# A quantised feed-forward kernel: 40 instead of 36 gate units finished during the up pass, with their magnitudes stored in DRAM

## The reference

```python
def act_qdq(x):
    qmax = 2.0 ** (ACT_BITS - 1) - 1.0
    scale = jnp.maximum(jnp.max(jnp.abs(x)) / qmax, 1e-12)
    return jnp.clip(jnp.round(x / scale), -qmax - 1.0, qmax) * scale
...
x = act_qdq(x)
up = act_qdq(x @ lpbq_dequant(w_up).T)
gate = act_qdq(x @ lpbq_dequant(w_gate).T)
sig = fixed_qdq_u16(jax.nn.sigmoid(gate))
gate = act_qdq(gate * sig)
o = act_qdq(gate * up)
return o @ lpbq_dequant(w_down).T
```

## Time and profile before

| | us |
|---|---|
| median of three runs | 2368.29 |
| profiled execution | 2368.93 |
| span of its trace | 2367.2 |
| TensorE busy in the span | 2019.6 |
| VectorE busy | 1708.7 |
| ScalarE busy | 1400.7 |

### The profile page before, as it was taken

How to read it: one execution, slowest core, us unless ns; L and a number is a source line. 1 busy time by engine, 2 the same in 40 slices (tenths; PEclk the granted TensorE clock), 3 DMA queues, 4 the chain that set the end, 5 groups by cost and what they waited for, 6 DMA issues and landing times.

```text
span 2367.2 us, 25402 instructions
## 1 busy us (share of the span) xinstructions
PE 2019.6 (85%) x9524; PEld 945.2 (40%) x9524; DVE 1708.7 (72%) x1372; ACT 1400.7 (59%) x1613; POOL 671.2 (28%) x665
## 2 busy tenths in 40 slices
PE   5688888888679999999999999999100699999998
PEld 2344444444334444444444444444000244444443
DVE  8699999999624534542399998999899745577641
ACT  2577878887522322232399987676899633366530
POOL 0499999999500000000022210222111000000000
PEclk9899999999889999999999999999555799999999
DMA  5879999999246755853599995787998755555541
GB/s 205 332 280 350 333 351 331 348 334 343 111 178 213 252 213 178 264 183 143 215 364 386 380 371 221 258 317 296 391 418 328 307 214 209 211 211 231 231 151 71
DMA packets 131163, 634.60 MB, mean 268 GB/s; under 512 B 12257, under 2 KB 12769, under 8 KB 91105
## 3 DMA queue, kind: packets, MB, share of 16 engines
q1 hardware_dynamic: 85888, 316.81, 36.8%
q0 software_dynamic: 45152, 316.16, 34.3%
HBM read 430.69 MB, written 202.24 MB: 267 GB/s over the span
## 4 chain that ended last, share of the span: by engine, by line
PE 63%; DVE 3%; issue 3%; ACT 2%; DMA 0%; POOL 0%; DVEq 0%; ACTq 0%; POOLq 0%
PE ff_pp L1640 42%; PE ff_pp L1654 21%; ACT ff_ring L1583 1%; DVE ff_sig L1437 1%; DVE ff_h_parts L1421 1%; DVE ff_sq L1359 1%; DMA ff_ab<-hT_scratch 0%; ACT ff_sig L1570 0%; DVE ff_sq L1428 0%; DVE kept_gate L1430 0%; DVE ff_gin L1372 0%; DVE ff_hq L1411 0%; ACT ff_hq L1494 0%; ACT ff_ring L1609 0%; ACT ff_sig L1599 0%
## 5 line engine op out<-in xcount | busy, mean ns | idle before, releaser
L1654 PE MATMUL ff_pp<-kept_down,kept_gate 128*128 128x512 f16 x1536 | 459.0, 381 | 193.1 <-DVE kept_up L1478 193.1
L1640 PE MATMUL ff_pp<-ff_h_parts,kept_gate 128*128 128x512 f16 x2304 | 499.7, 380 | 19.9 <-DVE ff_h_parts L1271 19.9
L1640 PE MATMUL ff_pp<-ff_h_parts,kept_up 128*128 128x512 f16 x2304 | 497.4, 379 | 0.0
L1501 ACT ACTIVATE ff_raw<-ff_pp 128x1024 f32<-128x1024 f32 x192 | 194.5, 1018 | 395.8 <-PE ff_pp L1640 395.8
L1640 PEld LDWEIGHTS ff_pp<-ff_h_parts,kept_gate 128*128 128x128 f16 x2304 | 225.9, 98 | 293.7 <-DVE ff_h_parts L1271 20.3
L1640 PEld LDWEIGHTS ff_pp<-ff_h_parts,kept_up 128*128 128x128 f16 x2304 | 225.4, 98 | 271.8
L1276 DVE TENSOR_REDUCE kept_gate_peak<-ff_raw 128x1 f32<-128x2048 f32 x48 | 109.7, 2286 | 292.5 <-ACT ff_raw L1501 292.5
L1654 PEld LDWEIGHTS ff_pp<-kept_down,kept_gate 128*128 128x128 f16 x1536 | 150.6, 98 | 376.0 <-issue 196.0
L1654 PE MATMUL ff_pp<-kept_down,kept_up 128*128 128x512 f16 x768 | 292.1, 380 | 0.0
L1609 ACT ACTIVATE ff_ring<-ff_hq,kept_g 128x2048 int16<-128x2048 f32 x48 | 96.0, 1999 | 191.1 <-DVE ff_hq L1411 189.7
L675 PE MATMUL at_psO<-kept_wo,at_ahi 128*128 128x512 f16 x512 | 153.9, 382 | 36.3 <-ACT at_alo L453 31.6
(11 more groups left out here) (239 smaller groups left out, 3446.7 us busy)
## 6 DMA issues: line engine op xcount, KB each, us to landing
ff_raw<-up_scratch SPq DMA_DIRECT2D x66, 1024.0 KB, 8.4
gate_scratch<-ff_raw POOLq DMA_DIRECT2D x48, 1024.0 KB, 6.5
ff_gin<-gate_scratch SPq DMA_DIRECT2D x48, 1024.0 KB, 8.8
up_scratch<-ff_raw POOLq DMA_DIRECT2D x48, 1024.0 KB, 7.0
ff_gin<-gate_integers SPq DMA_DIRECT2D x73, 512.0 KB, 6.0
gate_integers<-ff_ring POOLq DMA_DIRECT2D x43, 512.0 KB, 9.3
kept_up<-up_scratch SPq DMA_DIRECT2D x21, 1024.0 KB, 9.2
kept_xs<-in_x SPq DMA_DIRECT2D x32, 512.0 KB, 13.9
```

The lines of the kernel that those rows point to most:

```text
L1501: nc.scalar.activation(raw[:, n % UNITS, h * 2 * BLK:(h + 1) * 2 * BLK], pp[(2 * n + h) % 4][:, :, :].rearrange("p a t -> p (a t)"), ACT.C ...
L1640: mm = nc.tensor.matmul(pp[k % 4][:, h, :], wt[w][:, c, f:f + P], a[:, b % 2, :, c, :], start=(q == 0), stop=(q == len(todo) - 1))
L1654: mm = nc.tensor.matmul(pp[k % 8 // 2][:, k % 2, :], a[b % 2][:, f, t * P:(t + 1) * P], wt[w][:, f, :], start=(q == 0 and i == 0), stop=(q ...
```

## The change

READY goes from 36 to 40, so `second` starts at up unit 28 and 8 units are left "late". Magnitudes of 36 of the 40 are made in the up pass, at the unit in `MAG_AT`: two in most units from 31 on, one in unit 44, three in units 33, 46 and 47. For the 23 units that pass through the slots and are loaded again in the stretch of products (`passing`), ScalarE writes the magnitude into one of two tiles `ab`, and GpSimd's queue stores it (0.5 MB) in a new DRAM tensor behind the unit's other stores. The next magnitude in the same tile waits until that store has landed, and `load_again` waits for the magnitude before it fills a slot again. The stretch of products loads these magnitudes where it loaded integers. In it 36 units are "done", 8 "late", 3 "act" and 1 "dve" (before: 13, 12, 15 and 8).

```diff
-READY = 36
+READY = 40
...
-    DONE = list(range(KEPT)) + [v for v in range(KEPT, READY) if v - KEPT >= AGAIN - AR][:5]
     LOADED = AGAIN - AR
+    MAG_AT = {v: SECOND + ((3, 3, 4, 4, 5, 17, 18, 19)[v] if v < KEPT else v // 2 + 1 if v < KEPT + LOADED else v // 2 + 2)
+              for v in range(READY)}
+    DONE = sorted((v for v in range(READY) if MAG_AT[v] < NU), key=lambda v: (MAG_AT[v], v))
...
+        mag_out = [s.sem(f"mag_out{i}") for i in range(2)]
...
-            return [v for j, v in enumerate(DONE) if n == SECOND + max(3 + j if v < KEPT else 0, v // 2 + 2)]
+            return [v for v in DONE if MAG_AT[v] == n]
+
+        def passing(v):
+
+            return KEPT <= v < KEPT + LOADED
...
-            if made[i] == "done":
+            if home[i] == "load":
+                if made[i] == "done":
+                    have_gated(eng, i)
+                else:
+                    eng.wait_ge(m["ga_" + made[i]], nth(i) + 1)
+            elif made[i] == "done":
...
                             sp.wait_ge(again_out[w % AR], 16 * (w // AR))
+                            sp.wait_ge(m["mag"], DONE.index(KEPT + w - AR) + 1)
                         sp.dma_start(again(KEPT + w), gate_q[w]).then_inc(again_in[w % AR], 16)
...
+                def store_magnitude(v):
+                    w = v - KEPT
+                    pool.wait_ge(m["mag"], DONE.index(v) + 1)
+                    pool.dma_start(mag_d[w], ab[:, w % 2, :]).then_inc(mag_out[w % 2], 16)
...
+                        if j >= 2:
+                            pool.wait_ge(mag_out[j - 2], 16 * len(range(j - 2, LOADED, 2)))
                     if not late(u):
-                        pool.wait_ge(again_out[u % AR], 16 * (u // AR + 1))
-                    pool.dma_start(gated(i), gate_q[u]).then_inc(g_in[kind, j], 16)
+                        pool.wait_ge(mag_out[u % 2], 16 * (u // 2 + 1))
+                    pool.dma_start(gated(i), gate_q[u] if late(u) else mag_d[u]).then_inc(g_in[kind, j], 16)
...
                     for v in second_units(n - 1):
                         store_gated(v)
+                    for v in magnitude_at(n - 1):
+                        if passing(v):
+                            store_magnitude(v)
...
                 def magnitude(v):
 
+                    if passing(v):
+                        w = v - KEPT
+                        act.wait_ge(m["g2"], v + 1)
+                        if w < 2:
+                            act.wait_ge(m["gpeak"], NU)
+                        need(act, mag_out[w % 2], 16 * (w // 2))
+                        nc.scalar.activation(ab[:, w % 2, :], again(v), ACT.Abs).then_inc(m["mag"], 1)
+                        return
...
+    mag_d = nc.dram_tensor("gate_magnitudes", [NB * UNITS, P + 1, UE], I16).ap()[:, 0:P, :]
```

More of the change, by code:

```diff
@@ L772, in quantiser, with feed @@
     link(nc.vector.tensor_tensor(inv, inv, unit, ALU.mult))
-def feed(nc, keep, hT_d, hq_d, gate_d, up_d, gate_q, x1_d, out, NB, scale_d, mats):
+def feed(nc, keep, hT_d, hq_d, gate_d, up_d, gate_q, mag_d, x1_d, out, NB, scale_d, mats):
     g, al_ = keep["g"], keep["alpha"]
@@ L1702, in build @@
                     keep[n] = [keep[n + "_all"][:, i] for i in range(2)]
-                feed(nc, keep, hT_d, hq_d, gate_d, up_d, gate_q, x1_d, out, NB, scale_d,
+                feed(nc, keep, hT_d, hq_d, gate_d, up_d, gate_q, mag_d, x1_d, out, NB, scale_d,
                      [(up_n, up_t, "up", 5, F), (down_n, down_t, "down", 6, D)])
```

## The result

The changed kernel takes 2396.07 us (median of four runs, 2393.33 to 2397.33) against 2368.4, the median of four runs of the kernel before: a ratio of 1.0114 with an interval of 1.0101 to 1.0126, 27.7 us slower. The forecast was 2367 with a range up to 2382, so it was wrong in size and in sign. All three places where it put time did move, and in the directions it gave; two of the three sizes were off, both to the same side.

What follows compares the result with a forecast made beforehand. TensorE's matmuls carry the passes; in the 193.1 us hole ScalarE, VectorE and DMA engines are all full, and DMA would remain. Up pass 18, hole -24.5, restart 5 make -1.5 us: 2367, range 2353 to 2382.

Steps and rivals of the forecast that it cites:

- three places: Where the change was to count: up pass (18 us later), idle hole before the down pass (24.5 less), restart (5 more).
- The store loop: Up pass, units 34 to 44: magnitudes wait for earlier stores to land; two units take 16.2 us plus 6.5, costing 10.7.
- The block load: Up pass: `load_hq` stands behind magnitude waits, so VectorE stands some 3.5 us four times; counted half, 7 us.
- bound drawn for the lateness: Upper bound for the up pass's later end: landing 9.4, 12.8 us per unit, 26.7 + 5 = 32 us.
- The hole: Stretch from last eviction to last product, ended by DMA loads: 159 us instead of 183.5, a gain of 24.5.
- The head start: SP would start the hole's loads about 7.7 us ahead of the up pass's last eviction, because ScalarE is late.
- lower bound: Smallest gain in the hole: 20 us, if SP gets no head start and the DMA rate falls to 410.
- The restart: Start of the down pass: its first loads leave only near the end of the products, plus 5 us (4 to 6).
- Free stores: Rival: magnitude stores cost nothing in the up pass, landing near 4 us; -13 us, 2355; chance 0.15.
- VectorE did not end the hole: Denies the rival that VectorE, not the DMA engines, ends the hole; that rival's time 2359, -9 us, chance 0.12.
- The saturated loop: Rival: DMA engines full in units 34 to 44, landing 9.4, up pass 32 us later; +11, 2379; chance 0.23.
- the sum's 159: Forecast length of the hole: last load 152 us after the last eviction, 2.5 for the start, 4.3 for last product.

Runs made afterwards that it cites:

- experiment 7: Changed kernel with gate units loaded up to 12 products ahead instead of 7 (two magnitude tiles and late block load stay): 2387.93 us, ratio 1.0086.
- experiment 2: Changed kernel with the load of a block's integers issued two units earlier in SP's list, two magnitude tiles kept: 2384.85 us, ratio 1.0077.
- experiment 1: Changed kernel with four magnitude tiles instead of two, everything else as changed: 2380.38 us, ratio 1.0055.
- experiment 5: Changed kernel with four magnitude tiles, the block's integers loaded earlier, and gate units loaded up to 12 products ahead instead of 7: 2356.37 us, ratio 0.9951.
- experiment 6: Changed kernel with four magnitude tiles, early block load, 12 products of lead, and the down pass's first three up loads ahead of its gate loads: 2353.79 us, ratio 0.9941.
- the third experiment: Changed kernel with both four magnitude tiles and the early load of the block's integers: 2366.0 us, ratio 0.9991.

## Why the prediction was wrong

**What bounds the kernel.** Right in its three places. The share of 1.02 did set the time of the last load in the hole, some 154 us after the last eviction (forecast 152 and 2.5 for the start), and experiment 7 ran into it.

**The store loop.** The mechanism was right: which waits, in whose list, that two units take 16.2 us plus a landing. The step that failed is the value of that landing. Between 4.9 us at a DMA share of 0.81 and 9.4 at 0.99 the forecast took 6.5, "nearer to today's median, since the magnitudes leave in a burst after the raw store has landed". They landed in 8.7. The burst, which was to make it short, is how I read its length: the second finished unit, both magnitudes and a loaded unit are issued within a few microseconds, and each has the others ahead of it, even at a mean share of 0.86; no run takes the burst apart. With 8.7 the term of 10.7 us becomes 23, and experiment 2, where they landed in 9.0, measured 22.7.

**The block load.** Also named, and mis-sized twice. The load landed in 8.2 us instead of 5.5: the forecast read "4.5 to 8.8" from the earlier trace rows, but 8.8 is the median there, over the whole up pass, and 11.9 the longest. So VectorE stood 5.5 us each time instead of 3.5. And the forecast counted half, because it took the late peak to delay only every other unit. The chain above shows that it is a link of the same loop, and TensorE waited for the split as well, up to 7.0 us. The term of 7 is 14.9 by experiment 1. The bound drawn for the lateness, 32 us, had the landing at 9.4 but this term at 5; with 14.9 it would have held the 36.8.

**The hole.** The forecast let 4.3 us pass from the last load to the last product and treated the late units as part of VectorE's and ScalarE's work only. The step that failed is that one. Their loads leave seven products ahead (`NEAR`), their sigmoid is wanted three products ahead, so four products are left for the landing: at 3.6 us each enough before, at 2.2 us each, the pace the change makes possible, too short for a load of 8 us and more. ScalarE waited 19 us there, none before. That was a new wait that a faster engine called up, and the trace of before could not show it; the four products and the landing times were there to be compared. Experiments 5 and 7 gave 9 and 8 us back. The head start was there, 10.7 us (first up load at 1688.53) against 7.7. The forecast's lower bound was mis-added as well: its gain of 20 us leaves out the 2.5 and 4.3 us of its own sum, and with them it is 13. The measured gain of 12.0 comes near that by another way: neither of that bound's conditions held (a head start of 10.7, 415 GB/s from 1730 to 1830), the late units did it.

**The restart.** Right: 4.0 against 5, and experiment 6 shows the cause.

**The rivals.** Free stores fell with the 49.8 us that ScalarE waited for them (and that rival's gain of 21 in the hole lacks the same 6.8 us: 16.5, which makes its time 2360). VectorE did not end the hole either: it was busy 87.5 of the 100 us from 1730 to 1830. The saturated loop came nearest. Its lateness (32) was near, its time (2379) was not, since it took a hole of 157 us. Its condition, a landing from about 7.5 us on, held with 8.7; its reason, full DMA engines in the up pass, did not: the share was 0.86. The fit per DMA of the Trainium skill (DMA: Bandwidth & Descriptors, Anatomy of one DMA) makes an estimate of 3.2 us for such a store. No median here came near it: 4.9 in the kernel before, whose shortest took 3.7, 8.7 in the changed kernel, 13.3 in the third experiment.

**What was not tried.** The same magnitudes with READY at 36 were not tried. The hole of 163.8 us in experiment 7 stands 5 over the sum's 159 by the 10 us of VectorE behind the loads (4.3 in the sum); the 167.6 of experiment 5 had, besides, no head start (first up load 0.5 us ahead of the last eviction).

## What to carry to other kernels

A buffer that is emptied by a store into DRAM closes a loop through the landing time: add up one turn (queue position, landing, the work behind the wait) and compare it with the pace of the bounding engine times the units it spans; the number of tiles is chosen by that, and two more tiles were worth 22 us here. Take the landing time from a stretch with the same bursts, not from a median at a lower load. When an engine is made faster, recount in time every distance that the schedule states in units.

## What the runs showed of the hardware

TensorE's clock fell inside the up pass. After standing for 7.02 us until 1613.55 it ran the next matmuls at a granted clock of 0.59, a mean of the two levels (0.5 is 1.2 GHz, 1.0 is 2.4), and was back at 1.00 from 1620 on:

```profile
1606.00:1613.50 7.50, 0.53 (x3) 0.04 (x1) 1.93 (x3) 4.53 (x4) 0.46 (x1) 0.67 1.00 329
1613.50:1620.00 6.50, 6.45 (x18) 2.43 (x19) 6.46 (x4) 4.66 (x3) 0.49 (x1) 0.59 0.63 235
1620.00:1626.00 6.00, 6.00 (x29) 2.72 (x28) 5.82 (x4) 4.65 (x4) 3.19 (x5) 1.00 0.92 339
...
1654.53:1658.00 3.47, 3.47 (x9) 1.27 (x10) 3.44 (x3) 0.99 (x1) 0.00 (x0) 0.50 0.52 213
```

A second stop, of 6.96 us until 1654.53, was followed by 0.50 and by 1.00 again from 1660 on. A stop of 2.76 us until 1596.00 showed none of it (1.00 from 1590 to 1606). What the lower clock cost was not measured; the chain above runs through no matmul there. And stores of 0.5 MB took from 4.9 to 13.3 us to land in the median, at shares of 0.81 to 0.99, without a word of it in any engine's busy time.
